# Projection weights prepared by GpSimd in cross attention's last tile, ternary weights rounded by VectorE at the opening of the last stage

## The reference

```
x  = x + xattn(layernorm(x), ctx)      # self attention and cross attention over 1601
                                       # context rows, 16 heads of 128; both results
                                       # side by side (4096 columns), divided by a scale,
                                       # rounded to fp8, times wproj (256 x 4096)
x  = x + attn(layernorm(x))            # bitlinear layers (ternary weights, 8-bit input),
                                       # rotary block attention, gated feed-forward
x  = x + ffn(layernorm(x))             # ternary gate/up/down with scales by row
```

## Time and profile before

| what | value |
|---|---|
| median of 3 runs | 2562.75 us (2560.01 to 2563.15) |
| the profiled execution | 2561.66 us |
| its span, first to last instruction | 2559.8 us |
| busy share: PE, PEld, DVE, ACT, POOL | 89%, 72%, 76%, 61%, 55% |
| mean granted TensorE clock | 0.938 |
| cross attention's last output written | 2212.4 us |
| first instruction of the last stage's SyncE queue | 2217.7 us |

### The profile page before, as it was taken

The page is one execution under the profiler, slowest core; times in us unless marked ns, Lnnn a source line. Parts: engine busy times, 40 slices in busy tenths (PEclk is TensorE's granted clock), DMA queues, the critical chain, the costliest instruction groups (busy, mean ns, idle before and its releaser), DMA issues. The chain is left out here.

```text
span 2559.8 us, 49662 instructions
## 1 busy us (share of the span) xinstructions
PE 2266.5 (89%) x18258; PEld 1853.3 (72%) x18258; DVE 1937.3 (76%) x4402; ACT 1561.3 (61%) x3135; POOL 1405.7 (55%) x1537
## 2 busy tenths in 40 slices
PE   3868867999999999999999999999999999584666
PEld 1545656888888888888888888888888887362334
DVE  8988866777877777787777778777877877478753
ACT  5666645676777677677767767776776676211211
POOL 4334347776667677666767766676776655050000
PEclk8778879999999999999999999999999999786788
DMA  3112111101110111111011111101111000362100
GB/s 115 59 51 76 50 70 48 41 34 48 35 35 32 43 37 34 48 35 35 29 47 37 34 47 36 35 27 48 37 34 41 17 2 1 123 232 53 37 13 8
DMA packets 74478, 119.40 MB, mean 47 GB/s; under 512 B 21168, under 2 KB 56576, under 8 KB 73216
## 3 DMA queue, kind: packets, MB, share of 16 engines
q1 hardware_dynamic: 74240, 116.23, 13.4%
HBM read 94.20 MB, written 22.02 MB: 45 GB/s over the span
## 5 line engine op out<-in xcount | busy, mean ns | idle before, releaser
L75 PE MATMUL x_kc<-x_wk,x_ctxT 128*128 128x256 f16 x4992 | 623.3, 274 | 11.3 <-ACT x_sq L911 11.3
L75 PE MATMUL x_ox<-x_ctxp,x_pt 128*128 128x256 f16 x4992 | 609.6, 273 | 0.0
L681 POOL TENSOR_SCALAR x_kT<-x_kf 128x512 f16<-128x512 f32 (+1 forms) x448 | 282.2, 630 | 502.8 <-ACT x_kf L919 502.6
L75 PEld LDWEIGHTS x_kc<-x_wk,x_ctxT 128*128 128x128 f16 x4992 | 489.8, 98 | 82.7 <-ACT x_sq L911 14.5
L75 PEld LDWEIGHTS x_ox<-x_ctxp,x_pt 128*128 128x128 f16 x4992 | 484.3, 98 | 52.8
L683 POOL TENSOR_TENSOR x_kT<-x_kf,x_kT 128x512 f16<-128x512 f32 (+1 forms) x448 | 492.1, 1098 | 37.5
L1376 DVE TENSOR_TENSOR x_pt<-x_tp,x_pt 128x512 f16<-128x512 f32 (+1 forms) x512 | 288.9, 585 | 221.9 <-ACT x_pt L948 221.9
L1319 DVE TENSOR_REDUCE x_ss<-x_sq 128x4 f32<-128x512 f32 (+1 forms) x448 | 283.1, 644 | 170.1 <-ACT x_sq L911 169.6
L919 ACT ACTIVATE x_kf<-x_tp,x_hv 128x512 f32<-128x512 f32 (+1 forms) x448 | 331.8, 759 | 113.5 <-PE x_tp L1089 113.5
L907 ACT ACTIVATE x_kraw<-x_kc 128x512 f32<-128x512 f32 (+1 forms) x448 | 255.1, 569 | 150.8 <-PE x_kc L75 146.5
L948 ACT ACTIVATE x_pt<-x_tp 128x512 f16<-128x512 f32 (+1 forms) x512 | 259.3, 520 | 72.8 <-PE x_tp L1129 68.7
(11 more groups left out here) (246 smaller groups left out, 3048.4 us busy)
## 6 DMA issues: line engine op xcount, KB each, us to landing
x_stage<-in_ctxT SPq DMA_DIRECT2D x32, 800.5 KB, 4.4
x_stage<-in_ctx SPq DMA_DIRECT2D x16, 896.0 KB, 5.1
x_stage<-in_ctx SPq DMA_DIRECT2D x16, 640.0 KB
scr_q<-a_qxT SPq DMA_DIRECT2D x8, 1024.0 KB, 3.9
x_qs<-scr_q SPq DMA_DIRECT2D x16, 512.0 KB, 5.3
scr_core<-a_catc SPq DMA_DIRECT2D x8, 512.0 KB, 2.6
scr_x<-x_catx SPq DMA_DIRECT2D x8, 512.0 KB, 2.9
f_area<-in_wprojT SPq DMA_DIRECT2D x4, 1024.0 KB, 10.9
```

The lines of the kernel that those rows point to most:

```text
L75: last = pe.matmul(out, lhs[i], rhs[j], start=start and n == 0, stop=stop and n == len(parts) - 1)
L681: gp.tensor_scalar(dst[0], src, 1.0, 0.0, ALU.mult, ALU.add).then_inc(khi_ready, 1)
```

## The change

- **Projection weights.** In steps 2 to 5 of cross attention's last tile, the four "c" places of `POOL_ORDER` are each filled with `split_projection(n)`: GpSimd makes the high part and the rest of two of the 32 pieces (512 columns). SyncE loads each such piece (256 KB) with `load_projection(n)` into one buffer, `wpst`. That buffer lies at the end of `x_stage`; load n waits until the rest of piece n-1 has been written. The results lie where `x_stage`, `x_ctxT0` and `x_ctxp0` had their data, so these tensors now live on into the last stage (`kept`), and some of the last stage's own tensors (`hn`, `hg`, `hq`, `aT`, `bT`, `ident16`) lie in room that is left there. The fp32 loads of the last stage, ScalarE's rounding and VectorE's subtraction are gone. The identity matrix is kept too.
- **Ternary weights.** Their loads come right behind `load_cat(0)`. The loads of `f_scl` and `f_xr` move behind `load_cat(1)`. The nine rounding instructions go from GpSimd to VectorE (`ternary`), between the scales and `absorb(0)`.
- **TensorE** waits for `f_winv` before `project(3)`, and for nothing but `cat` in `project(0)`.

```diff
-        stage = xsb("stage", [P, 2, 7 * C])
-        ctxT = [xsb("ctxT0", [P, 2, KC, LP], F16)]
+        stage = lasting("stage", [P, 2, 7 * C])
+        ctxT = [lasting("ctxT0", [P, 2, KC, LP], F16)]
...
+        ctxp = [lasting("ctxp0", [P, 2, CH, C], F16)]
...
+        flat = stage[:].rearrange("p a n -> p (a n)")
+        wpst = flat[:, 3072:3584].rearrange("p (h n) -> p h n", n=C)
...
+                    if is_last(t) and 2 <= j < 6:
+                        for n in range(4):
+                            load_projection(4 * (j - 2) + n)
+
+            def load_projection(n):
+                if n == 0:
+                    sp.wait_ge(ctx_ready, 8 * B)
+                else:
+                    sp.wait_ge(wplo_ready, n)
+                sp.dma_start(wpst, a["wprojT"].rearrange("(h p) n -> p h n", p=P)[:, 2 * n:2 * n + 2, :]
+                             ).then_inc(wpst_ready, 16)
...
+            def split_projection(n):
+                hi, lo = (wp_unit[2 * (n // 4) + part][:, n % 4 * 512:(n % 4 + 1) * 512].rearrange("p (h n) -> p h n", n=C)
+                          for part in range(2))
+                gp.wait_ge(wpst_ready, 16 * (n + 1))
+                if n == 4:
+                    gp.wait_ge(kc_filled, (B - 1) * SPB * KU)
+                if n == 12:
+                    gp.wait_ge(pv_done, (B - 1) * G)
+                gp.tensor_scalar(hi, wpst, 1.0, 0.0, ALU.mult, ALU.add).then_inc(wphi_ready, 1)
+                gp.wait_ge(wphi_ready, n + 1)
+                gp.tensor_tensor(lo, wpst, hi, ALU.subtract).then_inc(wplo_ready, 1)
...
+                        if kind == "c" and is_last(t) and 2 <= j < 6:
+                            split_projection(4 * (j - 2) + n)
...
-            load_weights(0)
             load_cat(0)
-            for n in range(1, 4):
-                load_weights(n)
-            sp.dma_start(scl[:], a["scales"].partition_broadcast(P)).then_inc(scl_ready, 16)
-            sp.dma_start(xr[:], a["x"].rearrange("(t p) c -> p t c", p=P)).then_inc(x_in, 16)
...
             load_cat(1)
+            sp.dma_start(scl[:], a["scales"].partition_broadcast(P)).then_inc(scl_ready, 16)
+            sp.dma_start(xr[:], a["x"].rearrange("(t p) c -> p t c", p=P)).then_inc(x_in, 16)
             load_cat(2)
...
-            for t in range(1, 4):
+            for t in range(1, 3):
                 project(t)
             pe.wait_ge(winv_ready, 1)
+            project(3)
             a_turn(0)
...
+            def ternary(parts):
+                both = [(n, TERN[n][0], TERN[n][0] + TERN[n][1]) for n in parts]
+                for n, lo, hi in both:
+                    ins = v.tensor_scalar(tern_raw[:, lo:hi], tern_raw[:, lo:hi], winv[:, n:n + 1], INT_ROUND, ALU.mult, ALU.add)
+                c.done(ins)
+                for n, lo, hi in both:
+                    ins = v.tensor_scalar(tern_raw[:, lo:hi], tern_raw[:, lo:hi], INT_ROUND, 1.0, ALU.subtract, ALU.min)
+                c.done(ins)
+                for n, lo, hi in both:
+                    v.tensor_scalar(tern[:, lo:hi], tern_raw[:, lo:hi], -1.0, 0.0, ALU.max, ALU.add).then_inc(tern_ready, 1)
...
             ternary_scales()
+            ternary(range(3))
```

More of the change, by code:

```diff
@@ L606, in _ @@
             sp.wait_ge(xstored, TILES * 16)
+            sp.wait_ge(wplo_ready, 16)
             for s in used:
@@ L1627, in finish @@
         w_ready = sem("w_ready")
-        wst_ready = [sem(f"wst_ready{n}") for n in range(4)]
         cat_in = [sem(f"cat_in{n}") for n in range(NCAT)]
-        whi_ready = sem("whi_ready")
-        wlo_ready = sem("wlo_ready")
         ident_ready = sem("ident_ready")
@@ L2349, in build @@
     scr_x = nc.dram_tensor("scr_x", (TILES, P, NH * P), F16, kind="Internal").ap()
-    attend_self_and_cross(nc, a, scr_q, scr_core, scr_x)
-    finish(nc, a, scr_core, scr_x, out)
+    with ExitStack() as kept:
+        ident, wpj, free = attend_self_and_cross(nc, a, scr_q, scr_core, scr_x, kept)
+        finish(nc, a, scr_core, scr_x, out, ident, wpj, free)
 def rope_table():
```

98 lines of the change are left out of this document (39 added, 59 removed).

## The result

Seventeen executions of the changed kernel have a median of 2555.80 us, seventeen of the kernel before on the same chips one of 2561.76 (those beside the experiments, 15 to 21 each time, have medians of 2561.6 to 2562.0). The ratio is 0.9982, with a 95% interval of 0.9975 to 0.9988: faster by 3 to 6 us of 2560, just at the 0.2% that can be told from no change. The forecast was 2553.0. The change's own executions spread more than those of before (2553.92 to 2561.02 against 2560.01 to 2563.22); e11 shows a part of the reason.

What follows compares the result with a forecast made beforehand. The prediction took the last stage's opening, one queue of transfers at 353 KB per us, as the bound. From 2561.66 it took 12.5 and added 2.9 for cross attention's last tile: 2552.1, forecast as 2553.0 against the median, range 2545 to 2560.

Steps and rivals of the forecast that it cites:

- what is late next: Last stage's opening: project(3) needs cat 3, landing at 2251.6, so TensorE idles 4 us; project(3) ends at 2261.0.
- VectorE held by the fold, just under TensorE: Last stage's opening: GpSimd's fold holds VectorE until 2258.5; quantisation ends at 2260.5, just under TensorE's 2261.2.
- Relay 18.3: Last stage: from the first a_turn to the landing of the last of 12 loads, 18.3 us, which sets the rotation.
- Sum of the stage: 12.5: Last stage: the first rotation comes at 2279.5, a gain of 12.5 us carried to the end.
- from there on VectorE carries the chain: Last stage behind the first rotation: VectorE runs without a pause, so the 12.5 us gain reaches the end.
- The last tile: Cross attention's last tile: waits for single-buffer loads cost 0.7 us per step, 2.9 for four steps.
- 18.0 + 2L: Cross attention's last tile: microseconds from a step's start to its last key unit, L being a load's round trip, taken as 2.7.
- A: The forecast itself, whole kernel: 8 to 12 us gained, each limit being in the profile's rows; chance 0.45.
- Rival D: Cross attention's last tile: round trips of 3.3 to 4.2 give back most of the gain, 2558 to 2565; chance 0.12.
- My own sign of being wrong: Wrong if last-tile steps grow over 2 us each, roundings take over 9, or a new wait follows the first rotation.
- C: Last stage's opening: early fold and roundings delay VectorE by 3 to 5 us more, 2556.5; chance 0.15.
- E: Cross attention's last tile: round trips past 3.9 make the kernel slower, 2572 with 5.1; chance 0.08.

Runs made afterwards that it cites:

- e11: The changed kernel unaltered, run and profiled a second time: median 2555.22 us, ratio 0.9975 to the kernel before.
- e4: The changed kernel with the nine ternary rounding instructions back on GpSimd: median 2558.00 us, ratio 0.9981 to the kernel before.
- e2: The changed kernel with the fourth cat load ahead of the last feed-forward weights: median 2548.06 us, ratio 0.9946 to the kernel before.
- e6: The changed kernel with GpSimd's fold waiting until the first unit is quantised: median 2557.91 us, ratio 0.9988 to the kernel before.
- e1: The changed kernel with a second staging buffer, so load n waits for piece n-2: median 2549.91 us, ratio 0.9953 to the kernel before.
- e5: The changed kernel, one buffer, with the fourth piece behind GpSimd's last key unit in steps 2 to 5: median 2550.95 us, ratio 0.9960.
- e3: The changed kernel with both a second staging buffer and the fourth cat load early: median 2545.40 us, ratio 0.9931 to the kernel before.
- e9: e3 with the first turn and qkv product ahead of project(3), and the fold waiting for the second quantisation: median 2554.56 us, ratio 0.9970.

## Why the prediction was right, and where it was not

All times here are counted from the stage's first transfer, 2217.67 in the prediction's rows.

- **Landings at 353 KB per us.** `cat` 0 was forecast at 5.6 and landed at 4.9; the ternary weights 10.0 and 10.4; `cat` 3 33.9 and 34.1. One rate, read from the earlier trace rows, carried three landings to within 0.8.
- **`project(0)` at half clock, 9.4.** It took 9.25.
- **Nine roundings, 6 us, hidden beside `project(1)`.** They took 6 and ended with it. e4 shows that they cost nothing.
- **TensorE idle for 4, `project(3)` 9.4, first turn at 43.5.** It was idle for 5.87, because `project(2)` was done 1.5 earlier than I had it, and then took 9.98; the turn came at 44.05 (42.8 in e11). e2 took most of this wait away (1.32 was left) and gained 7 us, so it was the bound, as the prediction's "what is late next" said.
- **VectorE held by the fold, just under TensorE.** It ended the quantisation at 42.0 (42.8 forecast), and e6 shows that the hold-up decides nothing.
- **Relay 18.3.** 18.35, with VectorE waiting 6.27 for it.
- **Sum of the stage: 12.5.** 10.5 in the first profile (11.9 gained at the rotation and 1.4 lost behind it), and 13.2 in the second. The step "from there on VectorE carries the chain" is nearly true: TensorE's half clock lies on the path at a few places there.
- **The last tile: the term that was mis-sized.** 2.9 was forecast, and 10.5 and 9.7 were measured in two profiles; by the medians with and without the second buffer it is 5.9. The formula 18.0 + 2L holds in steps 2 to 4: in step 2 the two round trips were 3.84 and 2.80, which gives 24.6, and the keys were ready at 24.84. In steps 3 and 4, with L at 2.6 to 2.8, the loss was 0.78 and 1.06, against 0.7. In step 5 it is 1.0 short (23.8 against 24.89), by the held instruction shown in e1. Three more things were missing. The first wait of step 2 had an L of 3.8, that of step 5 one of 3.2, where I took one L for all from the only row of that size. In step 5 TensorE came to its scores 21.5 after the step's start instead of 22.68, as it has no raw keys left to compute there; the earlier trace rows show step 2, and I used them for all four. Behind a pause the clock fell, and in step 2 that cost 1.8, beside a pause of 2.14 where I had 0.7. The last 1.4 lie in the rest of the tile, with the low clock that comes and goes there.

The time came out at 2555.8, inside the range, 2.8 above the forecast. The gain is 6.0 against the 9.6 of the sum, and below the 8 to 12 of A. A's account of the opening stands; the shortfall is the tile's. Rival D named its cause, round trips of over 3.3, but for all eight, where in the profile of the change one was (3.84, and the next longest 3.23); what it has for their source, the semaphore from GpSimd to SyncE and back, took 0.11 of a round trip. The two profiled executions of the change, 2558.61 and 2559.20, lie in D's band, and the tile's loss in them lies within D's 7.6 to 14.8. My own sign of being wrong, steps that grow by more than 2 us each, showed in two of the four steps (3.97 and 3.28; 0.78 and 1.06 in the others). So the range held with some luck: with every execution as dear as the profiled one, the time would have come within 1.4 us of its end. C gives nearly the measured time and is not what happened: VectorE was not on the path. E's chain, a late load, late keys, an idle TensorE, ran past the 3.1 per step that E asks for in steps 2 and 5 only.

The Trainium skill (DMA: Bandwidth & Descriptors, Anatomy of one DMA and Bandwidth) had been set against this part: the estimate of 2.6 for 256 KB from its fit lies close to the 2.7 which the DMA issues of the changed kernel show as the median of the sixteen loads. As a median both are right, and neither could tell of the round trips of 3.8 in the change and 4.0 in e5. Its advice, fewer and larger transfers, is not what the runs ask for here: the same sixteen loads cost nothing once they are issued one piece earlier (tile 202.5 against 202.2). No run here tried larger ones.

## What to carry to other kernels

Work that is put into an idle engine is nearly free (e1: 0.3 us for 32 instructions) if its waits don't stand ahead of something that the busy engine needs, and if it doesn't lie beside instructions that it holds up. Cost a wait that repeats by its long draws and by the tightest of the places where it repeats, not by the median and the place that happens to be in view; or take it off the path, by a second buffer or by placing it behind the last thing that others wait for. When a block of transfers goes, look for the transfer that is late next and move it forward: here that was worth 7 us, more than the 6 of the whole change. One profiled execution can be a dear one: compare its time with the median before taking a gain from it, as I did not for e1 and e3. And before moving work out of a wait, make sure what that wait is for: e9 moved the fold out of a free place onto the path.

## What the runs showed of the hardware

- **A pause of TensorE can cost twice.** Behind pauses of 2.14 (the change) and 2.02 (e11) in step 2 the granted clock fell to 0.50, and the step lost 3.97 and 3.86; behind those of 1.71 and 1.96 (e6) it lost 1.87 and 2.11, and behind one of 0.83 (e4) 1.0, with the clock at 1.00. Where the step has other pauses the slower clock can be hidden: behind 3.50 in step 5 the clock was 0.52, and the step lost 3.28. How long the half clock lasts varies too: behind pauses of 5.87 and 5.60, `project(3)` took 9.98 and 8.46.
- **The round trip of a load through two engines has a tail, and the tail is the transfer's.** GpSimd's last write, the semaphore, SyncE's issue and the landing of 256 KB took 2.6 to 2.9 in 30 of the 40 waits of the change, e2, e4, e6 and e11, and 3.0 to 3.8 in ten, eight of them for the load behind a step's first piece; e5 had one of 4.0. The issue came 0.03 after the write and GpSimd's start 0.08 after the landing, in the long ones too. Why some transfers are long, no run shows.
- **GpSimd and VectorE take turns on long instructions with two inputs in SBUF.** In e9 three groups of VectorE went from 3.7 to 12.2 and the fold from 9.8 to 12.5: 13.5 us of work of the two, which side by side took 12.8. A one-input instruction is held as well: two of 256 columns took 6.41 in the change. The Trainium skill (SBUF — State Buffer, Who interferes with whom) says that the port pair which the two engines share is an exclusive lock for a whole instruction, taken by a VectorE instruction with two SBUF inputs or in a two-port mode. The rows of e9, with two inputs, agree with it; whether the held one-input instructions were in a two-port mode, no row shows.
